# ScalarE issues the maxima's transfers, and the maxima are turned a step earlier

## The reference

```python
x = x + 0.5 * ffn(layernorm(x), w_gate, w_up, w_down)     # FP4 quantised operands
x = x + attention(layernorm(x), Wq, Wk, Wv, Wo)
x = x + 0.5 * ffn(layernorm(x), w_gate, w_up, w_down)
```

```python
logits = jnp.einsum('bhqd,bhkd->bhqk', q, k) * scale
logits = jnp.where(causal_mask, neg, logits)
logits = logits - jnp.max(logits, axis=-1, keepdims=True)
e = jnp.exp(logits)
out = jnp.einsum('bhqk,bhkd->bhqd', e / jnp.sum(e, axis=-1, keepdims=True), v)
```

## Time and profile before

| | us |
|---|---|
| median of 3 runs | 2248.5 (2247.52 to 2252.72) |
| the profiled execution | 2248.54, its span 2246.8 |
| TensorE busy | 2057.4 (92% of the span) |
| VectorE busy | 1913.9 (85%) |
| ScalarE busy | 1289.7 (57%) |
| GpSimd busy | 1037.9 (46%) |

### The profile page before, as it was taken

One profiled execution on the slowest core, in us unless ns is written; L12 is line 12 of the kernel. 1 busy time (PEld: TensorE's weight loads), 2 busy tenths in 40 slices (PEclk: granted clock), 3 DMA queues, 4 the chain that ended last, 5 costly groups with the idle time before them and its releaser, 6 DMA issues. The chain is left out here.

```text
span 2246.8 us, 44426 instructions
## 1 busy us (share of the span) xinstructions
PE 2057.4 (92%) x13448; PEld 1346.1 (60%) x13448; DVE 1913.9 (85%) x4327; ACT 1289.7 (57%) x2221; POOL 1037.9 (46%) x1639
## 2 busy tenths in 40 slices
PE   4799999997998999989999899989996799999998
PEld 3688888886883333333333333333333778888887
DVE  6799999986987888888888888888872699999996
ACT  3455455543762766667766676666784345545552
POOL 4788888873664111111111111111111288888884
PEclk9999999997996999999999999999998899999998
DMA  6000000002689576677766677666624200000000
GB/s 208 1 1 0 0 0 0 0 1 77 229 242 171 77 130 117 123 120 122 130 119 124 114 124 129 118 123 119 122 79 152 70 13 21 19 19 19 19 19 24
DMA packets 163503, 184.92 MB, mean 82 GB/s; under 512 B 57696, under 2 KB 109280, under 8 KB 163040
## 3 DMA queue, kind: packets, MB, share of 16 engines
q1 hardware_dynamic: 163360, 183.17, 38.9%
HBM read 113.90 MB, written 85.98 MB: 89 GB/s over the span
## 5 line engine op out<-in xcount | busy, mean ns | idle before, releaser
L1438 ACT ACTIVATE probs<-hT_ps 128x512 f32<-128x512 f32 (+3 forms) x320 | 273.7, 855 | 214.4 <-PE hT_ps L1338 134.5
L1473 POOL TENSOR_SCALAR_AFFINE_SELECT diag_scores<-diag_scores 128x256 f32<-128x256 f32 (+1 forms) x192 | 94.5, 492 | 540.5 <-ACT diag_scores L1436 536.7
L1316 PE MATMUL gu_ps<-k_stack,q_stack 96*128 96x512 bf16 (+3 forms) x994 | 314.1, 349 | 15.1 <-DVE part_max L1509 8.7
L721 PE MATMUL gu_ps<-wguT_hi,ffn_xT_hi 128*128 128x512 f32 (+1 forms) x768 | 313.6, 408 | 7.6 <-DVE ffn_xT_lo L597 5.1
L1357 PE MATMUL gu_ps<-probs,v_group 128*17 128x512 f32 (+3 forms) x3072 | 317.9, 502 | 2.2 <-ACT probs L1438 1.1
L1509 DVE CUSTOM_DVE_ANT_0 gu_ps<-gu_ps,mask_qk 128x256 f32<-128x256 f32 x510 | 283.8, 583 | 36.8 <-PE gu_ps L1316 31.4
L721 PE MATMUL gu_ps<-wguT_hi,ffn_xT_lo 128*128 128x512 f32 (+1 forms) x768 | 290.8, 379 | 0.0
L721 PE MATMUL gu_ps<-wguT_lo,ffn_xT_hi 128*128 128x512 f32 (+1 forms) x768 | 290.3, 378 | 0.0
L1514 DVE TENSOR_REDUCE part_max<-gu_ps 128x1 f32<-128x512 f32 x352 | 233.3, 685 | 57.6 <-PE gu_ps L1316 57.2
L699 ACT ACTIVATE ffn_z<-xs,ffn_shift,ffn_rstd 128x256 f32 (+1 forms) x128 | 77.1, 602 | 350.5 <-POOL ffn_shift L650 350.5
L1438 ACT ACTIVATE probs<-av_ps 128x512 f32<-128x512 f32 (+3 forms) x320 | 275.1, 860 | 5.3 <-PE av_ps L1338 5.2
(11 more groups left out here) (207 smaller groups left out, 5133.0 us busy)
## 6 DMA issues: line engine op xcount, KB each, us to landing
q_stack<-q_parts SPq DMA_DIRECT2D x192, 128.0 KB, 7.1
k_stack<-k_parts SPq DMA_DIRECT2D x192, 128.0 KB, 7.6
o_all<-o_sb SPq DMA_DIRECT2D x64, 256.0 KB
q_parts<-qkv_parts SPq DMA_DIRECT2D x32, 384.0 KB, 2.7
k_parts<-qkv_parts SPq DMA_DIRECT2D x32, 384.0 KB, 2.8
v_ones<-qkv_vst SPq DMA_DIRECT2D x16, 544.0 KB, 3.8
v_group<-v_ones SPq DMA_DIRECT2D x32, 272.0 KB, 10.8
xs<-in_L_attn_x SPq DMA_DIRECT2D x8, 1024.0 KB, 12.0
```

The lines of the kernel that those rows point to most:

```text
L721: last = T.matmul(gu_ps[:, n, 0:cols.stop - cols.start], x[:, buf, k * P:(k + 1) * P], w[:, k, cols], start=k == 0 and m == 0, stop=k == K ...
L1316: mm = T.matmul(out[:, e, :], qs[0:STACK, h0 + e, t * P:(t + 1) * P], ks[0:STACK, h0 + e, c * CHUNK:c * CHUNK + w], start=True, stop=True)
L1438: S.activation(probs[:, pair, i % 2, :, first:w], scores[pair][:, :, first:w], ACT.Exp, scale=DH ** -0.5).then_inc(s[pr], 1)
L1473: G.affine_select(out=block_of, in_=block_of, compare_op=ALU.is_ge, fill=MASKED, base=0, pattern=[[0, 2], [0, count], [1, P]], channel_mul ...
```

## The change

ScalarE issues the two transfers, each at a place of its own in its order of instructions, and `MAX_STEP` becomes 5.

```diff
-            MAX_STEP = 6
+            MAX_STEP = 5
...
-                        def send_max(b, g):
-
-                            r = g % RING
-                            n = b * GROUPS + g
-                            once(sp, "m_lo", n, 1)
-                            once(sp, "m_hi", n, 1)
-                            slot = max_rows[bass.ds(n, 1), :, :].rearrange("o a c -> (o a) c")
-                            sp.dma_start(slot.rearrange("a (u q) -> u a q", q=P), mT[:, :, :]
-                                         ).then_inc(s["m_stored"], 16)
-                            sp.wait_ge(s["m_stored"], n * 16 + 16)
-                            sp.dma_start(ring[r][0][STACK:STACK_MAX, :, :].rearrange("p h t -> p (h t)"), slot
-                                         ).then_inc(max_loaded[r], 16)
-
...
-                        send_max(0, 0)
...
-                            nxt = later(b, g, 1, last)
-                            if nxt:
-                                send_max(*nxt)
...
+                        def store_max(b, g):
+
+                            n = b * GROUPS + g
+                            once(act, "m_lo", n, 1)
+                            act.dma_start(max_rows[n, :, :].rearrange("a (u q) -> u a q", q=P), mT[:, :, :]
+                                          ).then_inc(s["m_stored"], 16)
+
+                        def load_max(b, g):
+
+                            n, r = b * GROUPS + g, g % RING
+                            act.wait_ge(s["m_stored"], n * 16 + 16)
+                            act.dma_start(ring[r][0][STACK:STACK_MAX, :, :].rearrange("p h t -> p (h t)"),
+                                          max_rows[n, :, :]).then_inc(max_loaded[r], 16)
+
...
+                        store_max(0, 0)
+                        load_max(0, 0)
...
+                                if i == MAX_STEP + 2 and nxt:
+                                    store_max(*nxt)
+                                if i == MAX_STEP + 3 and nxt:
+                                    load_max(*nxt)
```

## The result

The changed kernel takes 2201.1 us (median of 4 runs, 2198.9 to 2202.8) against 2249.6 us: 0.9783 of before, 95% interval 0.9766 to 0.9800. The forecast was 2191 us (0.974) with a range of 2179 to 2216. The profiled execution took 2202.2 us with a span of 2200.2, 46.6 us less than before.

The account below looks back on a forecast made before the run. SP's loop of 31.26 us, longer than a group's 28.67, was taken to pace the attention. Terms of -66.7, +7 (reciprocal) and +2.5 (start) gave -57: 2248.5 to 2191 us, range 2179 to 2216.

Parts of the forecast that it names:

- SP's loop paces the attention, through its wait for the store: SP's queue: its turn of 31.26 us exceeds a group's 28.67 and makes the maxima's rows late; 66.7 us to gain.
- The new turn: SP's loop without the two issues and the wait: 27.9 us, 0.8 under a group's 28.67, so TensorE paces.
- The maxima leave earlier, TensorE's wait goes: Start of each group: the maxima's load lands at 1062.5, with 1.5 us to spare before TensorE's first scores.
- A new wait on ScalarE, priced at 0: ScalarE ahead of the load: a store landing within 3.5 us is free; bounds 0 and 4.1 us a group.
- the start: Ahead of the first group: four more units on VectorE start it 3.1 us later; cost 2.5 us.
- rival A: ScalarE stalls on the store: landing after 7.6 us, groups of 32.8 us, 2303 us in all; chance 0.06.
- The reciprocal: VectorE behind step seven's units: waits for the sums, 0.25 us a group, 7 us in all (0 to 35).
- The order of the units, priced at 0 with 0.2 us a group either way: VectorE's heaviest stretch comes one step earlier with the same work: 0, with 6 us either way.
- My clean group of before: A group of the kernel before whose start did not wait for the maxima's rows: 28.67 us.

Follow-up runs that it names:

- e1: Kernel before with ScalarE issuing the maxima's store and load, MAX_STEP left at 6: 0.9832 of before.
- e3: Kernel before with MAX_STEP 5, SP still issuing both transfers but the store ahead of the sums' load and the load behind it: 0.9791 of before.
- e2: Kernel before with only MAX_STEP changed from 6 to 5, SP issuing the transfers as before: 1.0000 of before.
- e4b: Changed kernel with SP holding the fourth set of loads until the first maxima's store landed, run again on a third chip: 2195.5 us, 0.9759 of before.
- e4: Changed kernel with SP holding the fourth set of loads until the first maxima's store landed: 2190.4 us, 0.9796 of before.
- e9: Kernel before, MAX_STEP still 6, with SP issuing the store ahead of the sums' load and the load behind it: 2201.1 us, 0.9768 of before.
- e11: Version e9 with the packing of the output moved from ahead of the maxima's load to behind it: 2197.0 us, 0.9749 of before.

## Why the prediction was right, and where it was off

- *SP's loop paces the attention, through its wait for the store.* Shown: take the wait out of its way, by ScalarE (e1) or by another order (e3), and a group takes 29.0 to 29.1 us; leave it and turn the maxima earlier (e2), and nothing is gained. The new turn was put at 27.9 us, the measured one is 29.04 in the group shown. The chain behind the sums' load was right, 1117.60 - 1109.80 = 7.8 us for a forecast of 7.8, with the reciprocal's wait in it. What is longer is the way from the loads to the sums' load, 19.40 us for 18.65, and the last part, 1.84 for 1.4, with a wait for the output's copy in it.
- *The maxima leave earlier, TensorE's wait goes.* Right for all groups but the first. Behind a wait the granted clock had fallen, and that loss goes with it. Measured on clean groups of 28.40 us, the 29 groups of before hold 51.1 us of waits and about 23.8 us more, which I put down to the clock (an estimate: the rest of 898.12 - 28 x 28.40 - 28.07). So over a quarter of what TensorE won back was clock. Which half of the change does it was not asked in the prediction: it is SP's queue freed of the wait; step five only gives the load more time, and what it costs in the groups is about what it gives.
- *A new wait on ScalarE, priced at 0.* Right for the groups: 2.4 us to landing in the middle. Of the sum's own terms the one mis-sized most is *the start*: 2.5 us forecast, 8.5 measured. Its reason was VectorE's four more units, and for these 3.1 us was right: with the loads held (e4b) the first group takes 32.04 us and ends a step (2.83 us) earlier than before's 31.72, so 3.15 more. What I left out is that SP, rid of the first `send_max`, issues the fourth set of loads ahead of the first store, and the store lands behind most of them, in 12.4 us: the first group is 39.41 - 32.04 = 7.4 us longer than with the loads held. That is rival A's mechanism, in one group of 32, and e4 shows it: 4.4 us with these loads held. The attention began 1.8 us earlier in this profile; its start lies anywhere from 713.6 to 717.9 us in the profiles of the kernels here, so that is no gain of the change, and it hides part of the loss.
- *The reciprocal.* 7 us forecast, 5.2 measured: between the third copy and the last, VectorE waited 9.1 us in 13 groups for the sums, and these groups are together 5.2 us over 28.80. So 5.2 / 9.1 = 0.6 of the wait was passed on to the group.
- *The order of the units, priced at 0 with 0.2 us a group either way.* A clean group takes 28.80 us with step five and 28.40 with step six (e1, e9, e11), so step five costs 0.4, 12 us in 29 groups, twice the bound. My clean group of before, 28.67, hid it, since it was not wholly clean: the kernel before had one of 28.40 too (778.05 - 749.65). What comes with step five are TensorE's weight loads that wait for the Exp, 0.9 us at most, 34.2 us in 41 places (33.4 in 40 in e2 and e3, but 7.0 in 9 with step six in e1); part of each lies beside the matmuls still running. That they make up the 0.4 us is likely, not shown.
- *The clock.* Three of the 29 groups take 30.17 us with no wait but the short ones that a clean group has too (0.44 us at the transpose); the granted clock's mean is 0.94 in the first of them and 1.00 in the group ahead. That is 3 x 1.37 = 4.1 us, forecast by nothing in my sum, and the kernel before had such a group as well.

```profile
870.70:899.50 28.80, 27.89 (x207) 10.45 (x205) 25.99 (x73) 21.66 (x36) 4.23 (x7) 1.00 0.74 130
899.50:929.67 30.17, 29.31 (x207) 10.73 (x205) 26.14 (x73) 21.72 (x36) 4.23 (x7) 0.94 0.71 125
```

- Together, against groups of 28.67: -66.7, +5.2 for the reciprocal, +28 x 0.13 = 3.6 for the order, +4.1 for the clock and -1.35 for the last group (27.32) give the 55.15 us of the 29 groups. Less the 8.5 us outside them, this is the 46.6 us of the span. The time came out 10 us over the forecast of 2191 (terms of the span): start +6.0, order +3.6, clock +4.1, less 1.8 at the reciprocal and 1.35 in the last group. Mechanism and direction were right; that the total stayed this near is in part these errors' not all having one sign.

## What to carry to other kernels

A queue that issues transfers is an engine like the others: add up its turn, with its waits, and compare it with the work that it feeds. A wait in it is moved or filled first, by issuing what must land ahead of a wait that stands there anyway; another issuer was not needed for that here. Ask also what the wait had covered: over half of SP's 92 us came back as a wait for the reciprocal. And when a wait is taken from a queue, look at what it now issues sooner, at the start above all, where the wait had also held something back.

## What was not expected of the hardware

- A small transfer, in each of the two queues tried beside SP's, landed about with the large ones issued before it: 12.4 us for 16 KB at the start, 7.5 and 9.6 us for 8 KB in a group, 0.15 to 0.20 us behind `sum_rows` at its end. At the start no packet of it ran in the first 8.7 of the 12.4 us.
- The same kernel's time differed by more than many a change is worth: before took 2234.8 us in the runs on one chip and 2252.5 us in those on another. Chip and time of the runs are not told apart here.
- TensorE's clock fell to its lower level, 1.2 GHz, for some 3 us (matmuls of 0.63 us in place of 0.38 at 903.75 us) in three groups of 29 in which TensorE had only the short waits of a clean group: 0.16, 0.44 and 0.26 us in the 3 us before the first of them.
